# Layer-0 attention chunks issued in another order, remote weighing and logits written by column groups

## The reference, cut to what matters

```python
xn = _layernorm(x)
# layer 0, attention: 16 heads of 8, windows of 32 tokens ("local"),
# and 8 heads over 64 pooled latents ("remote")
local = softmax(mask(Qb @ Kw.T / sqrt(8))) @ Vw
GQ = xn @ wgq; GK = pool(xn @ wgk); GV = pool(xn @ wgv)
rem = (softmax(mask(GQ @ GK.T / sqrt(8))) @ GV) @ r_out_w
gl, gr = sigmoid(Q . gate_local_w), sigmoid(Q . gate_remote_w)
x = x + (gl * local + gr * rem) @ w_out + top1_experts(xn, logits = xn @ wg)
# layer 1: linear attention and top-2 experts, logits = xn @ Wgate
```

## Time and profile before

| | us |
|---|---|
| median of 3 runs | 390.87 (390.83 to 391.59) |
| profiled execution | 389.36 |
| its span | 387.6 |
| PE busy in the span | 328.0 (85%) |
| DVE, ACT, POOL busy | 239.0, 181.3, 156.5 |

### The profile page before, as it was taken

One profiled execution on the slowest core, in us unless ns is written; L12 is line 12 of the kernel. 1 busy time (PEld: TensorE's weight loads), 2 busy tenths in 40 slices (PEclk: granted clock), 3 DMA queues, 4 the chain that ended last, 5 costly groups with the idle time before them and its releaser, 6 DMA issues.

```text
span 387.6 us, 10538 instructions
## 1 busy us (share of the span) xinstructions
PE 328.0 (85%) x3498; PEld 287.6 (74%) x3500; DVE 239.0 (62%) x760; ACT 181.3 (47%) x517; POOL 156.5 (40%) x215
## 2 busy tenths in 40 slices
PE   0887688789999898997987888999999999999900
PEld 0576567576999776766776447999999999999900
DVE  5728698777211366978778967866774444444417
ACT  1634355363654755634656843433334444444304
POOL 8211010737354405061212246454557886552320
PEclk9989899999999999999999989999999999999965
DMA  7782000101254120001111328887888988998137
GB/s 232 283 294 52 2 1 3 32 26 44 82 182 140 48 92 2 0 3 57 57 54 56 93 93 270 253 255 241 249 249 255 287 283 284 289 281 269 54 111 234
DMA packets 33204, 56.12 MB, mean 145 GB/s; under 512 B 4192, under 2 KB 11680, under 8 KB 33152
## 3 DMA queue, kind: packets, MB, share of 16 engines
q1 hardware_dynamic: 28704, 46.14, 37.8%
q0 software_dynamic: 3872, 8.27, 6.5%
q10 hardware_dynamic: 576, 1.05, 0.8%
HBM read 46.59 MB, written 8.85 MB: 143 GB/s over the span
## 4 chain that ended last, share of the span: by engine, by line
PE 62%; issue 14%; DVE 10%; ACT 4%; DMA 4%; POOL 4%; SPq 1%; DVEq 0%; ACTq 0%; POOLq 0%
PE bank L1316 18%; PE bank L1298 8%; PE bank L1325 4%; PE bank L1095 4%; PE bank L1081 4%; PE bank L1017 3%; PE bank L990 2%; PE bank L1005 2%; PE bank L1033 2%; DMA cb<-in_cb 2%; PE bank L1038 1%; PE bank L1271 1%; DVE rmax L1545 1%; PE bank L868 1%; PE bank L921 1%
## 5 line engine op out<-in xcount | busy, mean ns | idle before, releaser
L1316 PE MATMUL bank<-kf,shared 128*128 128x128 f32 x624 | 76.1, 275 | 0.0
L1316 PEld LDWEIGHTS bank<-kf,shared 128*128 128x128 f32 x624 | 73.3, 192 | 0.4
L557 POOL DMA_INDIRECT y_rows<-rows,to x39 | 38.8, 994 | 50.4 <-DVE rows L1808 49.6
L842 ACT ACTIVATE we<-bank,bcol 128x128 f32<-128x128 f32 x78 | 24.4, 363 | 53.8 <-PE bank L1316 53.8
L1801 DVE SCALAR_TENSOR_TENSOR we<-bank,bcol,we 128x128 f32<-128x128 f32 x78 | 23.8, 346 | 40.0 <-ACT we L842 39.9
L666 ACT ACTIVATE shared<-bank 128x512 f32<-128x512 f32 (+2 forms) x48 | 26.6, 554 | 45.6 <-PE bank L1038 22.8
L551 POOL DMA_INDIRECT rows<-xn_rows,from x39 | 38.0, 974 | 18.6 <-issue 11.7
L1545 DVE TENSOR_REDUCE rmax<-bank 128x8 f32<-128x512 f32 (+2 forms) x48 | 30.2, 629 | 23.2 <-PE bank L990 16.8
L1298 PE MATMUL bank<-xtT,shared 128*128 128x128 f32 x312 | 41.4, 276 | 0.8 <-ACT xtT L810 0.5
L1298 PEld LDWEIGHTS bank<-xtT,shared 128*128 128x128 f32 x312 | 38.0, 192 | 1.4 <-ACT xtT L810 0.8
L827 ACT ACTIVATE kexp<-bank,bcol 128x128 f32<-128x128 f32 x78 | 24.4, 363 | 28.9 <-PE bank L1298 28.9
(11 more groups left out here) (259 smaller groups left out, 677.1 us busy)
## 6 DMA issues: line engine op xcount, KB each, us to landing
shared<-in_w1s SPq DMA_DIRECT2D x39, 512.0 KB, 4.6
shared<-in_w1s SPq DMA_DIRECT2D x39, 256.0 KB, 4.1
we<-in_we SPq DMA_DIRECT2D x8, 514.0 KB, 3.4
xn_rows<-xn SPq DMA_DIRECT2D x12, 256.0 KB, 2.3
x<-in_x SPq DMA_DIRECT2D x4, 256.0 KB, 3.5
y_rows<-kf POOLq DMA_DIRECT2D x4, 256.0 KB, 7.3
w1s<-in_w1s SPq DMA_DIRECT2D x2, 512.0 KB, 8.3
xn<-y_rows SPq DMA_DIRECT2D x4, 256.0 KB, 3.7
```

The lines of the kernel that those rows point to most:

```text
L557: pool.indirect_dma_start(out=y1_rows, in_=ysb[:, i % 4, :], in_offset=None, out_offset=bass.IndirectOffsetOnAxis(ap=to1[:, i:i + 1].bitca ...
L842: last = act.activation(sil2[:, (k - 1) % 2, a, :], bank[(1, 3)[(k - 1) % 2]][:, P * a:P * a + P], ACT.Silu, bias=bias(e, 4 + a))
L1316: mm = pe.matmul(bank[(1, 3)[(k - 1) % 2]][:, P * f:P * f + P], wglb[:, (k - 1) % 4, a, P * f:P * f + P], zT2[:, (k - 1) % 2, a, :], start ...
```

## The change

On PE, `local_scores(g+2)` goes ahead of `queries(n+1)`; `weigh(g)` and `weigh(g+1)` go ahead of `remote_scores(g+4)`; `turn_remote` writes the last columns of bank 7 and so waits for the tanh of `gates`, no longer for the remote queries; `values(n+1)` waits for the remote queries (it waited for the copy of the turned remote output, in chunk 0 already for the remote queries). On ACT, the four head copies and the remote queries become `query_heads(n+1)` behind `latents(n)` and `keys(n+1)`, which swap places; `weighted(n,1)` goes ahead of `gates(n)`. On DVE, `mixed(n-1)` goes behind `spread` and `sums(n+1)`. Each remote `weigh` matmul becomes four of 32 stationary columns, over the 9 x REPS columns that are read; each logits matmul becomes four of 32 stationary columns.

```diff
--- before.py
+++ after.py
@@ -618,6 +618,8 @@
                 if n >= 2:
                     act.wait_ge(s_gates, n - 1)
                 act.copy(qT[:, n % 2, :], bank[6][:, 0:CH]).then_inc(s_qT, 1)
+
+            def query_heads(n):
                 if n >= 2:
                     act.wait_ge(s_S, U * (n - 2) + UL)
                 if n:
@@ -678,7 +680,7 @@
                 act.wait_ge(s_remt, n + 1)
                 if n:
                     act.wait_ge(s_rem, n)
-                act.copy(remT[:], bank[6][:, 0:P]).then_inc(s_remT, 1)
+                act.copy(remT[:], bank[7][:, CH:CH + P]).then_inc(s_remT, 1)
 
             def experts():
                 act.wait_ge(s_tx, 1)
@@ -715,6 +717,7 @@
             act.wait_ge(s_zero, 7)
             normalise(2)
             queries(0)
+            query_heads(0)
             act.wait_ge(s_k, 1)
             first_keys()
             normalise(3)
@@ -732,18 +735,19 @@
                     queries(n + 1)
                 exponent(g + 1)
                 act.wait_ge(s_k, n + 2)
+                latents(n)
                 if more:
                     keys(n + 1)
-                latents(n)
+                    query_heads(n + 1)
                 exponent(g + 2)
                 weighted(n, 0)
+                weighted(n, 1)
                 gates(n)
                 if n == 0:
                     gate_exp(0, tb[:], ta[:])
                 if n == NC - 1:
                     normalise1(1, range(4, 6))
                 exponent(g + 3)
-                weighted(n, 1)
                 if n:
                     remote(n - 1)
                 if n == NC - 1:
@@ -871,7 +875,8 @@
 
                 for n, t in enumerate(tiles):
                     pe.wait_ge(s_xTs, 4 * layer + t // 4 + 1)
-                    mm = pe.matmul(to[:, E * n:E * n + E], x_tile_T(t), w(name, E), start=True, stop=True)
+                    for part_ in range(0, P, 32):
+                        mm = pe.matmul(to[part_:part_ + 32, E * n:E * n + E], x_tile_T(t)[:, part_:part_ + 32], w(name, E), start=True, stop=True)
                 return mm
 
             def turn_x(i):
@@ -1030,8 +1035,10 @@
                     pe.wait_ge(s_ol, UL * n + u - 1)
                 for i in range(groups(g)):
                     if u >= UL:
-                        mm = pe.matmul(bank[4 + g % 2][:, P * i:P * i + P], probT[:, g % 2, P * i:P * i + P], gvd[REPS[n % NCH]][:, P * i:P * i + P],
-                                       start=True, stop=True)
+                        wide = VW * REPS[n % NCH]
+                        for part_ in range(0, P, 32):
+                            mm = pe.matmul(bank[4 + g % 2][part_:part_ + 32, P * i:P * i + wide], probT[:, g % 2, P * i + part_:P * i + part_ + 32],
+                                           gvd[REPS[n % NCH]][:, P * i:P * i + wide], start=True, stop=True)
                         continue
                     at = 4 * (u // 2 * 2 + i % 2) + u % 2 * 2 + i // 2
                     for hh in range(HG):
@@ -1041,8 +1048,8 @@
 
             def turn_remote(n):
                 pe.wait_ge(s_or, UG * n + UG)
-                pe.wait_ge(s_gq, min(n + 3, NC))
-                pe.transpose(M0[:, 0:P], remn[:], ident).then_inc(s_remt, 1)
+                pe.wait_ge(s_tg, min(n + 2, NC))
+                pe.transpose(M1[:, CH:CH + P], remn[:], ident).then_inc(s_remt, 1)
 
             def remote(n):
                 pe.wait_ge(s_tg, min(n + 2, NC))
@@ -1138,9 +1145,9 @@
                     logits0(3).then_inc(s_lg, 1)
                 if n == NC - 1:
                     turn_x1(0)
+                local_scores(g + 2)
                 if more:
                     queries(n + 1)
-                local_scores(g + 2)
                 turn(g + 1)
                 if n and n != FFN0_AFTER + 1:
                     weigh(g - 1)
@@ -1156,16 +1163,14 @@
                     keys(n + 1)
                 latents(n).then_inc(s_k, 1)
                 turn(g + 2)
+                if n == 0:
+                    pe.wait_ge(s_lgread, 1)
+                weigh(g)
+                weigh(g + 1)
                 remote_scores(g + 4)
-                weigh(g)
                 gates(n)
                 turn(g + 3)
                 remote_scores(g + 5)
-                if n == 0:
-                    pe.wait_ge(s_lgread, 1)
-                weigh(g + 1)
-                if n == NC - 1:
-                    pe.wait_ge(s_xTs, 5)
                 if n:
                     turn_remote(n - 1)
                 weigh(g + 2)
@@ -1175,14 +1180,12 @@
                     pe.wait_ge(s_tg, 1)
                     prefix(0)
                 if n == NC - 1:
+                    pe.wait_ge(s_xTs, 5)
                     turn_x1(1)
                 turn(g + 4)
                 if more:
                     local_scores(g + 6)
-                    if n:
-                        pe.wait_ge(s_remT, n)
-                    else:
-                        pe.wait_ge(s_gq, 2)
+                    pe.wait_ge(s_gq, n + 2)
                     values(n + 1)
                 weigh(g + 3)
                 turn(g + 5)
@@ -1657,9 +1660,7 @@
                 if n == 1:
                     one_hot_slots(10, 5)
                 shift(g + 5)
-                if n:
-                    mixed(n - 1)
-                else:
+                if n == 0:
                     place()
                 if n == 1:
                     one_hot_slots(T, 10)
@@ -1671,7 +1672,9 @@
                     spread(slice(8, 12))
                 if more:
                     sums(n + 1)
-                if n == 0:
+                if n:
+                    mixed(n - 1)
+                else:
                     slot_factors(0, T, J0)
                 if more:
                     shift(g + 6)
```

## The result

| | before | after |
|---|---|---|
| median (range) of 4 runs each, us | 390.85 (389.36 to 391.59) | 380.14 (376.79 to 383.28) |
| ratio, 95% interval | | 0.970 (0.962 to 0.978) |
| profiled execution, its span, us | 389.36, 387.6 | 379.0, 377.1 |
| mean granted clock of that execution | 0.966 | 0.959 |

The account below looks back on a forecast made before the run. PE was taken to bound chunks 2 and 3, sharing chunks 1 and 6 with DVE. Chunk-by-chunk gains, switch and new waits deducted, total 11.7 us: 389.4 to 377.7 profiled, median 379.2, range 372.5 to 385.7.

Parts of the forecast that it names:

- The third shift: DVE in chunk 0: starts at 26.2 instead of 29.51, as logits shorten and local scores precede queries; gain 3.3 us.
- Latents first with the weighs ahead: PE's `remote_scores` in all eight chunks: 1.56 us of cover removes a wait of 1.2 each, 9.0 us in all.
- The tanh: `turn_remote` on PE would wait for it 0.6 to 1.0 us in chunks 1, 4, 5; 1.6 put against.
- The wait for `mixed` in chunk 7: PE's `project` would wait 2.7 us behind DVE's statistics and spread; net gain 0.4 for the chunk.
- REPS 2: Remote weigh in four chunks: 0.89 to 0.38 us each, twice a chunk, 4.1 us in all.
- switch: PE entering 32-column matmuls: 0.15 us per change of form, eight more entries, 1.2 us against.
- REPS 8: Remote weigh with 72-column parts: 0.22 against 0.10 us by records, but no gain taken.
- The copy's wait: PE's 3.5 us wait for the copy of the turned remote output: left as it is, though it may go.
- Parts not side by side: Rival for weighing and logits: column parts cost 0.028 us a record and save nothing; 384.3 us, chance 0.10.
- parts dearer than what they replace: Rival for weighing and logits: above 0.040 us a record the kernel is slower, 398.5 at 0.055; chance 0.05.
- ACT as the new bound: Rival: later ACT steps from latents to tanh hold `turn_remote` about 1 us in seven chunks; 385.2 us, chance 0.16.
- Gain not passed on: Rival: the stage behind the chunks is held by something that doesn't start sooner; no change, 391 us, chance 0.04.

Follow-up runs that it names:

- x_wback: Changed kernel with both weighs back behind the remote scores on PE and the second weighted copy back behind the tanh's exponent on ACT: 382.08 us, ratio 0.977.
- x_qfirst: Changed kernel with the queries put back ahead of the local scores on PE: 381.50 us, ratio 0.976 to the kernel before.
- x_mixall: Changed kernel with `mixed` back ahead of spread and sums on DVE in every chunk: 376.21 us, ratio 0.960 to the kernel before.
- x_wide: Changed kernel with remote weighing and logits back to whole 128-column matmuls, the new order kept: 384.97 us, ratio 0.983 to the kernel before.
- x_after: The changed kernel run again, nothing altered, to see how far its times spread: 381.18 us, ratio 0.973 to the kernel before.
- x_cols: Kernel before with only the column parts added (remote weighing and logits), old order kept: 387.68 us, ratio 0.992 to the kernel before.
- x_mix7: Changed kernel with `mixed` back ahead of statistics and spread on DVE in chunk 7 alone: 375.15 us, ratio 0.958 to the kernel before.
- x_warm: Changed kernel plus unread matmuls filling three PE stands (ends of chunks 0 and 1, ahead of chunk 7's projection): 375.59 us, ratio 0.957 to the kernel before.

## Why the prediction was right, and where its steps were not

The prediction was right in total, by steps some of which missed in both directions. That the total came within 1 us is partly luck: a wait that it left standing went (3.1 us), and a move whose cost it had put at the wait alone brought a slow clock as well. Chunk by chunk, in us gained between the same PE steps as in the earlier trace rows, with chunk 3 taken to the start of the experts (predicted, then measured in the first profile): chunk 0 3.3, 4.0; chunk 1 0.9, 0.0; chunk 2 1.8, 1.2; chunk 3 2.05, 3.0; experts 0.5, 0.6; chunk 4 0.6, 0.9; chunk 5 0.7, 1.1; chunk 6 1.4, 1.2; chunk 7 0.4, -0.5. That is 11.65 predicted, and 11.6 measured if the parts aren't rounded; the span lost 10.5, as the start ran 0.5 later and the tail 0.6 longer in this execution.

*Right.* The third shift was put at 26.2 and came at 26.16. Latents first with the weighs ahead cover the whole wait of `remote_scores`, and x_wback shows that it takes both. The local scores ahead of the queries count in chunk 0 and not in PE's chunks (x_qfirst). The tanh becomes a wait in chunks 1, 4 and 5, of 0.60, 1.01 and 0.60, and in no other. The wait for `mixed` in chunk 7 was put at 2.7 and is 2.55; the 1.51 in chunk 6 was not named, and x_mixall, which hasn't got it, gains nothing there. Chunk 6 is DVE's.

*The price of the parts.* REPS 2 was right, 0.38 against 0.89, at a switch of 0.08 to 0.09 instead of 0.15. The switch back costs up to 0.10 as well, which was not put (keys behind a weigh 0.59, not 0.49). REPS 8, for which nothing was put, loses 0.13 to 0.24 a weigh; a record costs more with more columns: 0.012, 0.017 and 0.033 us for 18, 36 and 72. REPS 4 gains 0.10 after the switch. Chunk 3 holds two REPS 2 weighs: 0.85 predicted, 0.69 in x_wide against x_after and 0.65 in x_cols against before. The logits were put at 1.1 and took 0.92.

*The order's own share was larger, through the term left at nothing.* The copy's wait was left as it is (3.5, "the copy still follows an exponent on ACT"); it fell to 0.4. In chunk 3 the order alone (before 17.81, x_wide 15.53) brings 2.28: the wait of `remote_scores` 1.2, that of the copy 0.7, and 0.4 of PE's own time. That is why chunk 3 gained 3.0 and not 2.05. The step that failed took the rank of the copy on ACT for its time: its place behind an exponent is the same, but that exponent comes sooner. Here is the exponent, the copy and its matmul in chunk 3, first before, then after:

```profile
91.45 0.60 ACT L666 ACTIVATE shared<-bank 128x512 f32<-128x512 f32 x1 [1.36 <-PE bank L1038]
92.04 0.28 ACT L681 COPY remT<-bank 128x128 f32<-128x128 f32 x1
92.47 0.46 PE L1053 MATMUL bank<-remT,wts 128*128 128x128 f32 x2 [0.70 <-ACT remT L681]
```

```profile
84.07 0.61 ACT L668 ACTIVATE shared<-bank 128x512 f32<-128x512 f32 x1
84.75 0.27 ACT L683 COPY remT<-bank 128x128 f32<-128x128 f32 x1
85.16 0.46 PE L1060 MATMUL bank<-remT,wts 128*128 128x128 f32 x2
```

`exponent(g+3)` writes the half of the probabilities that `weigh(g+1)` reads, and so waited 1.36 us for it, as that weigh stood behind the remote scores. The weigh now stands ahead of them: the exponent follows the tanh without a wait and ends at 84.68, `turn_remote` at 84.71, and the copy is done ahead of its matmul. In x_wback the exponent waits 1.37 for the weigh again, and the copy's wait is back. The range had named that these 3.5 "may go".

*Chunk 7 was mis-sized.* The wait was right; the slow clock behind it was left out, and the savings set against it were too large. Logits, two weighs and the first `keys_values` now run behind the spread and not beside it: x_mix7 and x_warm price that at 2.6, about the wait itself, and 1.4 to 1.5 more by the clock, most of it behind the window's end. Against a predicted net of +0.4 the chunk lost 0.5. Without this one move (x_mix7) it takes 13.30 us between the same steps and gains 2.3, not the 3.6 that was counted as saved: the wait of 1.1 for a shift stands ahead of 177.34, and so in chunk 6, and one of the two weighs stands behind the window's end.

*The clock was left out where stands grew or chunks closed up.* The prediction used it for chunk 0, rightly: the stretch to the third shift fell by 3.8, of which the logits are 1.7 (x_wide), the queries 1.05 (x_qfirst), and the rest, 1.05, fits the low clock: the scores took 1.92 us at 0.50 and take 1.05 now. But it took chunk 2 as free of it, and in the first profile the clock fell there to 0.53: 16.22 us instead of the 15.2 to 15.5 it had named; in x_after, where it did not fall, the same steps take 14.71, less than was named, as the copy's wait goes here too. In chunk 1 the gain of 0.9 was to come from scores ahead of slow queries. The scores do go first, but the clock fell a little later than before (0.88 over the first 2 us, 0.50 before), and the scores took 1.92 us from 42.17. The slow queries now stand ahead of the remote weigh, and DVE stands 1.10 us for it (the row at 46.63), behind the 1.83 that it stood for the scores; before it stood 2.56 once. The gain there was 0.0.

*The rivals.* Parts not side by side (0.028 a record) and parts dearer than what they replace (break-even at 0.040): the two frequent forms run at 0.012 and 0.010, and only the 72-column form, 32 records of all, reaches 0.033. The Trainium skill, TensorE: Matmul & The Clock Gate, section "Wait — 56ns, not 53.3ns?", has about 25 ns as the closest that matmuls start to each other; the 0.010 and 0.012 us measured here for parts that write different column groups don't agree with it. That counts records; by whole f32 matmuls, two records each, it is 0.019 us for the logits and 0.024 for the weighs, just below it. ACT as the new bound: `turn_remote` waits 2.2 us in three chunks and never in chunks 2, 3, 6 and 7, so no. Gain not passed on: the second layer's experts start 10.6 us earlier and end 10.5 us earlier.

## What to carry to other kernels

Before a move that makes an engine wait is accepted, list what is queued behind the waiting instruction on that engine: in chunk 7 a wait of 2.55 us cost 4.1, as all the work behind it came 2.6 later and then ran at a slow clock for 1.5 more. A wait that you leave "as it is" deserves the same: ask what the engine ahead of it waits for, and whether the change moves that. A stand of PE can be dearer than its length if PE-bound work follows; fill it with useful work, or with useless work, and compare executions by stretch and by granted clock before a difference of 1% is believed. Splitting a matmul into four column parts pays where the parts are narrow (8 and 18 columns here), brings 0.10 us a weigh at 36, and loses at 72.

## What the runs showed of the hardware that was not expected

The clock's fall behind a stand is not certain. The same program had it at chunk 2 in one execution (1.00 became 0.53 behind a stand of 1.50 us) and not in the next, and the kernel before ran through 62.77 to 65.77 at 1.00. A stand of 3.0 us at the start of chunk 1 was followed by a fall in after (0.72 from 41 to 47 us) and in x_after (0.74), and by none in x_warm and x_mix7 (1.00 from 42 to 48 and from 41 to 47), the first with its stand filled, the second with one of 1.44 us, behind a fall that had come earlier (0.66 from 36 to 41 us), where DVE's chain hid it. Why a fall comes in one execution and not in another, these runs don't settle. Over whole runs, the kernel before took 389 to 392 us at a mean clock of 0.966 and 394 to 395 at 0.953.
